# A routed layer on one Trainium2 core: the table of tokens and weights moves into four extra columns of each routed row

## Chip, cores and metric

The kernel runs on one core of one Trainium2 chip. The metric is the device time of one execution in microseconds (us), lower is better.

## What is computed

The reference is a transformer layer on 8192 tokens (16 sequences of 512) of width 256, all in float32:

```python
x = L0_attn_inputs_q
xn = _layernorm(x, axis=-1)
x = x + attn(xn) + ffn(xn)
```

`attn` is linear attention with 16 heads. `ffn` is a shared SwiGLU block plus a routed part: each token picks one of two groups of four experts, then the best two experts in it, with a weight for each.

```python
h = _swiglu(flat @ w1.T)
for e in range(NUM_EXPERTS):
    routed = routed + h * w_se[:, e:e + 1] @ w2[e].T
```

So every token has one hidden row `h` of 512 numbers, two experts and two weights.

## The kernel before

**Matmuls.** Each float32 operand is split into a high part and a low part, and each product is made of three matmuls (`mm3`, lines 341 to 343). TensorE (PE) does little else.

**First phase, 16 batches of 512 tokens** (`batch` on each engine, unrolled for the first and the last, a loop between). In one batch PE computes keys, values, queries, the shared hidden layer and the routed hidden layer, and closes with the output products `y` (lines 599 to 615). VectorE (DVE) makes `kb`, the routing (`probabilities`, `best_two`, `ranks_in`, `table_rows`) and all gates. The two experts of a token form one of 12 classes. `ranks_in` gives each token its place in the list of its class, so `pos_i` is its row in a DRAM table with room for `CAP` = 8320 rows in each class. Two DRAM tensors are filled at that row by GpSimd (POOL), with indirect transfers of 128 rows each:

- `tab_d` takes 16 bytes per token: token number, two weights, a zero (tile `rows`);
- `h_d` takes the hidden row, 2048 bytes (buffers `hs[t]`, which lie over `phik` and `expt`).

POOL's order in a batch is written by hand. In the first batch it is: `low(0)`, `low(1)`, the split of `w_out`, four table scatters (line 1222), `reciprocal_root(1)`, `biased()` (adds the bias to the residual, line 1200), four row scatters (line 1228), `low(2)`, `low(3)`. The functions `low` make `h_lo` (line 1176), which PE needs for `y`. In the later batches `reciprocal_root` and `biased` stand at the start of the batch.

The next batch's normalised input `xn` goes to DRAM and back in another layout on the SP queue (lines 394 and 397), and DVE transposes it into `xT` (`x_transposed`, line 840), which lies over `phik`; so `x_transposed` waits for two things: the loads of line 397 (`xn_ld`) and the landing of the four row scatters (`hs_st`). After `xT` SP loads the input of the batch after (line 377), DVE takes its statistics (`norm`, line 809) and only then does `base` and `k_in` (line 940).

**Unused rows.** The second phase works on tiles of 128 rows, and the last tile of a class is only partly filled. So `tab_d` is filled at the start, 13 transfers of a constant (token 8192, which is out of bounds and is skipped), lines 366 to 368, on the SP queue behind the weights; and `h_d` gets 13 transfers of zeros behind the end of each class, in the last batch (line 412).

**Second phase, 75 tiles of 128 rows.** Each tile has one pair of experts. SP (first half) and ScalarE (ACT, second half) load a tile of `h_d` in four pieces of 128 x 512 bytes (`pieces`, line 348), DVE transposes it (line 1096), ACT makes the high part, DVE the low part (line 1102), PE multiplies with both experts, DVE scales with the weights (`add`, lines 1128 and 1130), POOL adds the rows to `out` with an indirect transfer (line 1274). The weights and tokens of a tile come with a load of 128 x 16 bytes from `tab_d` (line 432). SP works in groups of four tiles, and a group begins with a wait for the table loads of the groups before:

```python
def tiles_in(q):
    wait_apart(sp, tab_ld, 16 * TB * q)
```

Of the kernel before, what the change touches and what calls it, by code (L numbers as in the profile page):

```python
# [6 lines left out]
def layer_program(nc, x, w_k, w_v, w_q, w_o, w_in, w_out, w_exp, w_rt, b_q, b_kl, b_o,  # L7
# [7 lines left out]
    P = 128  # L15
# [19 lines left out]
    ROWS = SENT + P  # L35
    H1 = 512
    W1 = 2 * 1024
    UNIT = E * HC * D // B
# [4 lines left out]

    h_d = nc.dram_tensor("h_d", (ROWS, H1), f32, kind="Internal").ap()
    tab_d = nc.dram_tensor("tab_d", (ROWS, 4), i32, kind="Internal").ap()
    xn_d = nc.dram_tensor("xn_d", (S, D), f32, kind="Internal").ap()

    ctx = ExitStack()
    with ctx:
# [6 lines left out]
        def pair(name, shape):  # L56
# [16 lines left out]
        kb = sb("kb", [P, TB, D], f32)  # L73
        expt = sb("expt", [P, 2, 512], f32)
        relut = sb("relut", [P, 2, 512], f32)
        phik = sb("phik", [P, TB, D], f32)
        v = sb("v", [P, TB, DC, QG, HP + 1], f32)
# [59 lines left out]
        tok = sb("tok", [P, TB], f32)  # L137
        rows = sb("rows", [P, TB, 4], i32)

        fill = wexp_hi[:, W1 + B * UNIT - 4 * CAP // P:].bitcast(i32).rearrange("p (n w) -> p n w", w=4)  # L140
        cnt_i = sb("cnt_i", [P, NSLOT], i32)
# [6 lines left out]
        ends = wstage[0:1, 4 * NT:4 * NT + NSLOT].bitcast(i32)  # L148
        zeros = wstage[:, 512:1024]
        tab = wstage[:, 0:4 * NT].bitcast(i32).rearrange("p (n w) -> p n w", w=4)  # L150
        cur = sb("cur", [P, 2, TB, 4], i32)
        idx_cur = sb("idx_cur", [P, 2, TB], i32)

        hs = [phik[:, 0:2, :].rearrange("p t d -> p (t d)"), phik[:, 2:4, :].rearrange("p t d -> p (t d)"),
              expt[:, 0, :], expt[:, 1, :]]

        xn_blocks = xt[:, :, :].rearrange("p t d -> p (t d)").rearrange("p (b c k) -> p b c k", c=DC, k=32)
        xT = phik[:, :, :].rearrange("p t d -> p (t d)").rearrange("p (c s) -> p c s", c=DC)

# [33 lines left out]
        w_ld = sem("w_ld")  # L193
        fill_st = sem("fill_st")

# [3 lines left out]
        w1_split = sem("w1_split")  # L199
        fill_set = sem("fill_set")  # L200
        const_set = sem("const_set")
# [64 lines left out]
        hlo_rdy = sem("hlo_rdy")  # L266
        row_st = sem("row_st")
        hs_st = sem("hs_st")
# [83 lines left out]
        def _(sp):  # L352
# [11 lines left out]

            sp.wait_ge(fill_set, 2)
            for c in range(NCLS):
                sp.dma_start(tab_d[c * CAP:(c + 1) * CAP, :].rearrange("(p n) w -> p n w", p=P), fill[:, :, :]).then_inc(fill_st, 16)
            sp.dma_start(tab_d[SENT:ROWS, :], fill[:, 0, :]).then_inc(fill_st, 16)

            def load(b, last):  # L370
# [30 lines left out]

            sp.wait_ge(zero_set, 1)
            sp.wait_ge(ends_rdy, 1)
            for n in range(NCLS + 1):
                if n < NCLS:
                    g, k = divmod(n, NCLS // 2)
                    j, i = PAIRS[k]
                    end = sp.value_load(ends[0:1, 16 * g + 4 * j + i:16 * g + 4 * j + i + 1], min_val=0, max_val=SENT)
                    tail = bass.ds(end, P)
                else:  # L410
                    tail = slice(SENT, ROWS)
                sp.dma_start(h_d[tail, :], zeros).then_inc(zero_st, 16)

            sp.wait_ge(wexp_split, B)
            sp.wait_ge(infoi_rdy, 1)
            sp.wait_ge(zero_st, 16 * (NCLS + 1))
            sp.wait_ge(fill_st, 16 * (NCLS + 1))
            sp.wait_ge(row_st, 16 * TB * B)
            sp.wait_ge(hs_st, 16 * TB * B)
            sp.wait_ge(xT_rdy, 2 * (B - 1))  # L420

            def tiles_in(q):

                wait_apart(sp, tab_ld, 16 * TB * q)
                rows_at = rows_of(mybir.EngineType.SP, q * TB, TB)
                for t in range(TB):
                    at = rows_at[t]
                    if first_row(q) and t == 2:
                        sp.wait_ge(qlo_rdy, DC * B)
                    wait_apart(sp, tr_done, TB * q + t - 3)  # L430
                    pieces(sp, at, t, 0)
                    sp.dma_start(tab[:, bass.ds(q * TB + t, 1), :].rearrange("p t w -> p (t w)"),
                                 tab_d[bass.ds(at, P), :]).then_inc(tab_ld, 16)

# [7 lines left out]
        def _(pe):  # L442
            def first_transposes():

                pe.wait_ge(stay_ld, 16)
                for t in range(TB):
                    pe.wait_ge(xn_rdy, t + 1)
                    for c in range(DC):
                        mm = pe.transpose(bank[2 + 2 * c][:, t * P:(t + 1) * P], phik[:, t, c * P:(c + 1) * P], ident)
                        if t == TB - 1:  # L450
                            mm.then_inc(t_done, 1)
# [27 lines left out]
            def batch(b, last):  # L479
# [37 lines left out]
                for c in range(DC):  # L517
                    for t in range(TB):
                        for n in range(QG):
                            at = c * P + n * HP  # L520
                            mm = pe.matmul(bank[2][n * HP:(n + 1) * HP, c * (HP + 1):(c + 1) * (HP + 1)], phik[:, t, at:at + HP],
                                           v[:, t, c, n, :], start=(c == 0 and t == 0), stop=(t == TB - 1), skip_group_check=True)
# [264 lines left out]
        def _(dve):  # L787
# [30 lines left out]
            def first_normalise():  # L818
                dve.wait_ge(rstd_rdy, 1)
                for t in range(TB):  # L820
                    dve.tensor_scalar(phik[:, t, :].rearrange("p (c i k) -> p c i k", c=DC, k=32),
                                      xt[:, t, :].rearrange("p (i c k) -> p c i k", c=DC, k=32),
# [85 lines left out]
            def table_rows(b):  # L908

                wait(dve, row_st, 16 * TB * b)  # L910
                wait(dve, hs_st, 16 * TB * b)
# [23 lines left out]
            def batch(b, last):  # L935
# [7 lines left out]
                def phi_k(i):  # L943
                    dve.wait_ge(ek_rdy, 2 * b + i + 1)
                    wait(dve, acc_done, b)
                    wait(dve, hs_st, 16 * TB * b)
                    dve.scalar_tensor_tensor(phik[:, 2 * i:2 * i + 2, :].rearrange("p t n -> p (t n)"),
                                             kb[:, 2 * i:2 * i + 2, :].rearrange("p t n -> p (t n)"), 0.0,
# [212 lines left out]
        def _(pool):  # L1161
            pool.memset(fill[:, :, 1:4], 0).then_inc(fill_set, 1)
            pool.memset(fill[:, :, 0:1], N).then_inc(fill_set, 1)
            pool.memset(mhalf[:, :], -0.5).then_inc(pool_set, 1)
# [27 lines left out]
            def batch(b, last):  # L1192
# [15 lines left out]
                if last:  # L1208
                    pool.wait_ge(wexp_split, B)
                    pool.memset(zeros, 0.0).then_inc(zero_set, 1)  # L1210
                low(0, HC * b, hhi_rdy, hlo_rdy)
                low(1, HC * b + 1, hhi_rdy, hlo_rdy)

                if first_row(b):
# [3 lines left out]
                    low_part(wstage[:, :], wout_hi_, wout_lo_, ffn_split)  # L1218
                    pool.wait_ge(fill_st, 16 * (NCLS + 1))
                wait_apart(pool, row_rdy, b + 1)  # L1220
                for t in range(TB):
                    scatter(tab_d, rows[:, t, :], t, row_st)
                if first_row(b):
                    reciprocal_root(1)
                    biased()
                for t in range(TB):
                    wait_apart(pool, rg_rdy, TB * b + t + 1)
                    scatter(h_d, hs[t], t, hs_st)
                low(2, HC * b + 2, hhi_rdy, hlo_rdy)
# [132 lines left out]
```

## Time and profile before

| | us |
|---|---|
| median of 3 runs | 936.19 |
| lowest, highest | 934.6, 937.14 |
| the profiled execution, its own time | 936.16 |
| its span, first to last instruction | 934.3 |

The mean granted TensorE clock over the span is 0.989 of full speed. The profile is one execution; the span leaves out 1.9 us that lie around it. Times in its rows count from the start of the span.

### The profile page before, as it was taken

What the parts mean: (1) busy time and instruction counts of PE and PEld (TensorE: products, weight loads), DVE (VectorE), ACT (ScalarE), POOL (GpSimd) and SP (SyncE); (2) the same over time, 40 slices, a digit from 0 to 9 for tenths busy, and PEclk for the clock granted to TensorE, in tenths of its full rate; (3) what the DMA queues carried; (4) which work ended last, traced back from release to release, by engine and by line L of the source; (5) the groups of instructions that cost most, each with busy time, mean ns of one, the idle gap of its engine ahead of it and who ended that gap; (6) DMA issues with size and microseconds to landing.
All of it is one profiled execution on the core that took longest, in us unless ns stands there. A gap on an engine that the chain in (4) does not pass through costs nothing. (4 is left out here: it accounts for less than half of the span.)

```text
span 934.3 us, 22822 instructions
## 1 busy us (share of the span) xinstructions
PE 907.5 (97%) x6974; PEld 818.6 (88%) x6975; DVE 697.6 (75%) x1819; ACT 363.4 (39%) x596; POOL 464.9 (50%) x554
## 2 busy tenths in 40 slices
PE   7879999999999999999999999999989999999995
PEld 7678989898898989898888989898969999999995
DVE  5958687877878686877778786877675877777773
ACT  4425445344535345454435354453431222222220
POOL 4754364535354453635253543645352556655564
PEclk8999999999999999999999999999999999999998
DMA  9133324241313224241313223241155777787760
GB/s 277 59 113 103 123 61 138 61 123 68 101 68 101 93 76 146 57 134 48 120 68 101 90 79 131 60 134 55 60 192 132 144 136 142 144 151 137 136 125 1
DMA packets 145912, 100.21 MB, mean 107 GB/s; under 512 B 55520, under 2 KB 136928, under 8 KB 145888
## 3 DMA queue, kind: packets, MB, share of 16 engines
q1 hardware_dynamic: 105600, 64.08, 24.0%
q0 software_dynamic: 17968, 25.32, 12.6%
q10 hardware_dynamic: 22320, 10.51, 4.1%
q8 instruction: 13, 0.21, 0.1%
q14 instruction: 11, 0.09, 0.0%
HBM read 53.29 MB, written 48.00 MB: 108 GB/s over the span
## 5 line engine op out<-in xcount | busy, mean ns | idle before, releaser
L341 PE MATMUL bank<-wexp_hi,xnT_hi 128*128 (+1 forms) x560 | 191.1, 341 | 2.3 <-DVE phik L933 1.6
L343 PE MATMUL bank<-wexp_hi,xnT_lo 128*128 (+1 forms) x560 | 186.1, 332 | 0.0
L342 PE MATMUL bank<-wexp_lo,xnT_hi 128*128 (+1 forms) x560 | 185.8, 332 | 0.0
L1176 POOL TENSOR_TENSOR h_lo<-gated,h_hi 128x256 fp32r<-128x256 f32 x128 | 97.1, 779 | 104.0 <-ACT h_hi L683 103.6
L341 PEld LDWEIGHTS bank<-wexp_hi,xnT_hi 128*128 128x128 f32 x560 | 106.3, 190 | 15.7 <-issue 4.2
L343 PEld LDWEIGHTS bank<-wexp_hi,xnT_lo 128*128 128x128 f32 x560 | 106.3, 190 | 10.7
L342 PEld LDWEIGHTS bank<-wexp_lo,xnT_hi 128*128 128x128 f32 x560 | 106.4, 190 | 9.6
L341 PE MATMUL bank<-xnT_hi,win_hi 128*128 128x512 f32 x256 | 102.4, 400 | 3.1 <-DVE expt L933 3.1
L1200 POOL TENSOR_TENSOR res<-res,bo_t 128x256 f32<-128x256 f32 x64 | 47.2, 766 | 113.5 <-DMA res<-x 113.5
L343 PE MATMUL bank<-xnT_hi,win_lo 128*128 128x512 f32 x256 | 100.4, 392 | 0.0
L342 PE MATMUL bank<-xnT_lo,win_hi 128*128 128x512 f32 x256 | 100.3, 392 | 0.0
L341 PE MATMUL bank<-wexp_hi,h_hi 128*128 x296 | 83.4, 282 | 0.1
L343 PE MATMUL bank<-wexp_hi,h_lo 128*128 x296 | 83.3, 281 | 0.0
L342 PE MATMUL bank<-wexp_lo,h_hi 128*128 x296 | 83.2, 281 | 0.0
L1274 POOL DMA_INDIRECT out<-res,idx_cur x39 | 61.4, 1574 | 42.2 <-DVE res L1130 31.4
L1195 POOL DMA_INDIRECT tab_d<-rows,pos_i x64 | 63.2, 987 | 37.9 <-DVE tok L925 21.2
L683 ACT CAST h_hi<-gated 128x512 fp32r<-128x512 f32 x64 | 39.7, 620 | 108.0 <-DVE gated L929 108.0
L341 PE MATMUL bank<-wout_hi,h_hi 128*128 128x256 f32 x256 | 72.9, 285 | 3.7 <-POOL h_lo L1176 3.7
L929 DVE TENSOR_TENSOR gated<-gated,bank 128x512 f32<-128x512 f32 x64 | 43.9, 685 | 43.7 <-ACT gated L679 43.7
L341 PE MATMUL bank<-wkv_hi,xnT_hi 128*128 128x266 f32 (+1 forms) x256 | 73.9, 289 | 2.5 <-DVE xnT_lo L834 1.3
L342 PE MATMUL bank<-wkv_lo,xnT_hi 128*128 128x266 f32 (+1 forms) x256 | 73.4, 287 | 0.0
L343 PE MATMUL bank<-wkv_hi,xnT_lo 128*128 128x266 f32 (+1 forms) x256 | 73.3, 286 | 0.0
(191 smaller groups left out, 2417.2 us busy)
## 6 DMA issues: line engine op xcount, KB each, us to landing
res<-x SPq DMA_DIRECT2D x16, 512.0 KB, 3.6
out<-res SPq DMA_DIRECT2D x16, 512.0 KB, 3.0
xt<-x SPq DMA_DIRECT2D x15, 512.0 KB, 3.5
xn_d<-xt SPq DMA_DIRECT2D x15, 512.0 KB, 4.7
xt<-xn_d SPq DMA_DIRECT2D x60, 128.0 KB, 3.2
xt<-h_d SPq DMA_DIRECT2D x76, 64.0 KB
xt<-h_d ACTq DMA_DIRECT2D x76, 64.0 KB
kb<-h_d SPq DMA_DIRECT2D x76, 64.0 KB
```

The lines of the kernel that those rows point to most:

```text
L341: e.matmul(to, w_hi, m_hi_, start=first_, stop=False, skip_group_check=free)
L342: e.matmul(to, w_hi, m_lo_, start=False, stop=False, skip_group_check=free)
L343: return e.matmul(to, w_lo, m_hi_, start=False, stop=last_, skip_group_check=free)
L683: act.copy(h_hi[:, j, :], gated[:, j % 2, :]).then_inc(hhi_rdy, 1)
L929: dve.tensor_tensor(gated[:, j % 2, :], gated[:, j % 2, :], bank[up_bank][:, :], ALU.mult).then_inc(gate_rdy, 1)
L1176: ins = pool.tensor_tensor(h_lo[:, j, cols], gated[:, j % 2, cols], h_hi[:, j, cols].bitcast(f32), ALU.subtract)
L1195: pool.indirect_dma_start(d, bass.IndirectOffsetOnAxis(ap=pos_i[:, t:t + 1], axis=0), src, None).then_inc(done, 16)
L1200: ins = pool.tensor_tensor(res[:, t, :], res[:, t, :], bo, ALU.add)
L1274: pool.indirect_dma_start(out, bass.IndirectOffsetOnAxis(ap=idx_cur[:, t // TB, t % TB:t % TB + 1], axis=0), ring[t], None, bounds_check=N ...
```

## The change

The row of `h_d` grows from 512 to 516 numbers. Columns 512 to 515 hold what `tab_d` held. In SBUF one tile `hrow` of 4 x 516 numbers per partition takes the place of `phik`, `expt` and `rows`. One indirect transfer writes hidden row, token and weights. `tab_d`, its fill and the four table scatters of each batch are gone. The transfers behind the ends of the classes write rows of 516 numbers, whose token is 8192 and whose other numbers are zero. The second phase reads the pieces and the table entries from the wider rows. The diff, cut to its core (names of `phik[:, t, ...]` that become `phik(t)[:, ...]` are left out):

```diff
+    HR = H1 + 4
...
-    h_d = nc.dram_tensor("h_d", (ROWS, H1), f32, kind="Internal").ap()
-    tab_d = nc.dram_tensor("tab_d", (ROWS, 4), i32, kind="Internal").ap()
+    h_d = nc.dram_tensor("h_d", (ROWS, HR), f32, kind="Internal").ap()
...
-        expt = sb("expt", [P, 2, 512], f32)
+        hrow = sb("hrow", [P, TB, HR], f32)
+        expt = hrow[:, 2:4, 0:H1]
...
-        rows = sb("rows", [P, TB, 4], i32)
+        rows = hrow[:, :, H1:HR].bitcast(i32)
...
-        zeros = wstage[:, 512:1024]
+        tails = wstage[:, 1024 - HR:1024]
...
+        hs = [hrow[:, t, 0:H1] for t in range(TB)]
+        def phik(t):
+            return hrow[:, t // 2, (t % 2) * D:(t % 2 + 1) * D]
...
-        xT = phik[:, :, :].rearrange("p t d -> p (t d)").rearrange("p (c s) -> p c s", c=DC)
+        xT = hrow[:, 0:DC, 0:S]
...
-            sp.wait_ge(fill_set, 2)
-            for c in range(NCLS):
-                sp.dma_start(tab_d[c * CAP:(c + 1) * CAP, :].rearrange("(p n) w -> p n w", p=P), fill[:, :, :]).then_inc(fill_st, 16)
-            sp.dma_start(tab_d[SENT:ROWS, :], fill[:, 0, :]).then_inc(fill_st, 16)
...
-                sp.dma_start(h_d[tail, :], zeros).then_inc(zero_st, 16)
+                sp.dma_start(h_d[tail, :], tails).then_inc(zero_st, 16)
...
                     sp.dma_start(tab[:, bass.ds(q * TB + t, 1), :].rearrange("p t w -> p (t w)"),
-                                 tab_d[bass.ds(at, P), :]).then_inc(tab_ld, 16)
+                                 h_d[bass.ds(at, P), H1:HR].bitcast(i32)).then_inc(tab_ld, 16)
...
-            pool.memset(fill[:, :, 1:4], 0).then_inc(fill_set, 1)
-            pool.memset(fill[:, :, 0:1], N).then_inc(fill_set, 1)
...
-                    pool.memset(zeros, 0.0).then_inc(zero_set, 1)
+                    pool.memset(tails[:, 0:H1], 0.0).then_inc(zero_set, 1)
+                    pool.memset(tails[:, H1:H1 + 1].bitcast(i32), N).then_inc(zero_set, 1)
+                    pool.memset(tails[:, H1 + 1:HR], 0.0).then_inc(zero_set, 1)
...
-                    pool.wait_ge(fill_st, 16 * (NCLS + 1))
                 wait_apart(pool, row_rdy, b + 1)
-                for t in range(TB):
-                    scatter(tab_d, rows[:, t, :], t, row_st)
...
-                    scatter(h_d, hs[t], t, hs_st)
+                    scatter(h_d, hrow[:, t, :], t, hs_st)
```

## Rows read from the trace of the kernel before

**Rows 1.** Page, busy time of TensorE.

```profile
PE 907.5 (97%) x6974; PEld 818.6 (88%) x6975; DVE 697.6 (75%) x1819; ACT 363.4 (39%) x596; POOL 464.9 (50%) x554
```

**Rows 2.** Waits of PE: in total, times, longest.

```profile
PE bank L341 <- POOL h_lo L1176: 3.7, 1, 3.7
...
PE bank L341 <- DVE lg L941: 1.2, 1, 1.2
...
PE bank L341 <- DVE xnT_lo L1102: 0.7, 1, 0.7
```

**Rows 3.** Page, costliest groups: the table scatters.

```profile
L1195 POOL DMA_INDIRECT tab_d<-rows,pos_i x64 | 63.2, 987 | 37.9 <-DVE tok L925 21.2
```

**Rows 4.** Timeline of POOL, first batch: start, duration, what, idle before.

```profile
41.22 1.21 POOL L1195 DMA_INDIRECT tab_d<-rows,pos_i  x1 [0.18 <-issue]
...
47.37 3.02 POOL L1200 TENSOR_TENSOR res<-res,bo_t 128x256 f32<-128x256 f32 x4
...
54.75 0.96 POOL L1195 DMA_INDIRECT h_d<-expt,pos_i  x1 [0.30 <-issue]
```

**Rows 5.** Timeline of DVE, first batch and start of the second.

```profile
43.52 0.69 DVE L1015 TENSOR_TENSOR qn_hi<-relut,stay 128x512 fp32r<-128x512 f32 x1
...
47.42 3.12 DVE L828 TENSOR_SCALAR xt<-xt,mv,rstd 128x256 f32<-128x256 f32 x4
...
60.47 1.30 DVE L840 STREAM_TRANSPOSE phik<-xt 128x512 f32<-128x512 f32 x2 [7.45 <-DMA h_d<-expt,pos_i]
...
68.80 0.42 DVE L940 TENSOR_TENSOR kb<-bank,bkl 128x256 f32<-128x256 f32 x1
```

**Rows 6.** Line 828 in all batches: min/median/max ns.

```profile
L828 DVE TENSOR_SCALAR xt<-xt,mv,rstd x60: 402/405/880, 47.4 to 621.4; 128x256 f32<-128x256 f32 x60
```

**Rows 7.** Timeline of the SP queue, first batch.

```profile
50.57 0.38 SPq L394 DMA_DIRECT2D xn_d<-xt  x1
53.53 2.09 SPq L397 DMA_DIRECT2D xt<-xn_d  x4
62.03 0.41 SPq L377 DMA_DIRECT2D xt<-x  x1
```

**Rows 8.** DMA issues, 53.5 to 61 us: count, KB, median us to landing.

```profile
xt<-xn_d SPq DMA_DIRECT2D x4, 128.0 KB, 4.3
```

**Rows 9.** The same, 161 to 167 us, a middle batch.

```profile
xt<-xn_d SPq DMA_DIRECT2D x4, 128.0 KB, 3.1
```

**Rows 10.** Windows: busy us (instructions) by engine, PEclk, DMA share, GB/s.

```profile
57.20:59.90 2.70, 2.70 (x12) 2.70 (x13) 0.00 (x0) 0.00 (x0) 2.62 (x5) 0.50 0.82 188
```

**Rows 11.** The same for 40 us of the second phase.

```profile
760.00:800.00 40.00, 40.00 (x338) 40.00 (x337) 30.10 (x57) 8.69 (x14) 26.85 (x22) 1.00 0.76 140
```

**Rows 12.** Timeline of the SP queue, second phase.

```profile
723.96 0.88 SPq L348 DMA_DIRECT2D xt<-h_d  x2
...
780.66 0.86 SPq L348 DMA_DIRECT2D xt<-h_d  x2
...
787.01 0.37 SPq L432 DMA_DIRECT2D wstage<-tab_d  x1
...
791.58 0.86 SPq L348 DMA_DIRECT2D xt<-h_d  x2
...
823.28 0.86 SPq L348 DMA_DIRECT2D xt<-h_d  x2
```

**Rows 13.** Timeline of DVE, second phase, two tiles eight apart.

```profile
781.43 0.49 DVE L1128 TENSOR_SCALAR res<-bank,cur 128x256 f32<-128x256 f32 x1 [0.68 <-PE bank L343]
...
804.32 0.48 DVE L1128 TENSOR_SCALAR res<-bank,cur 128x256 f32<-128x256 f32 x1 [0.68 <-issue]
```

**Rows 14.** Waits of the SP queue from 716 to 925 us.

```profile
SPq L293 <- DMA wstage<-tab_d: 35.1, 15, 3.1
```

**Rows 15.** DMA issues, 2 to 8.3 us, two loads at the start.

```profile
expt<-w_q SPq DMA_DIRECT2D x1, 256.0 KB, 4.2
...
bkl<-b_kl SPq DMA_DIRECT2D x1, 133.0 KB, 4.0
```

More of the change, by code:

```diff
@@ L73, in layer_program @@
         kb = sb("kb", [P, TB, D], f32)
-        expt = sb("expt", [P, 2, 512], f32)
+        hrow = sb("hrow", [P, TB, HR], f32)
+        expt = hrow[:, 2:4, 0:H1]
         relut = sb("relut", [P, 2, 512], f32)
-        phik = sb("phik", [P, TB, D], f32)
         v = sb("v", [P, TB, DC, QG, HP + 1], f32)
@@ L137, in layer_program @@
         tok = sb("tok", [P, TB], f32)
-        rows = sb("rows", [P, TB, 4], i32)
-        fill = wexp_hi[:, W1 + B * UNIT - 4 * CAP // P:].bitcast(i32).rearrange("p (n w) -> p n w", w=4)
+        rows = hrow[:, :, H1:HR].bitcast(i32)
         cnt_i = sb("cnt_i", [P, NSLOT], i32)
@@ L152, in layer_program @@
         idx_cur = sb("idx_cur", [P, 2, TB], i32)
-        hs = [phik[:, 0:2, :].rearrange("p t d -> p (t d)"), phik[:, 2:4, :].rearrange("p t d -> p (t d)"),
-              expt[:, 0, :], expt[:, 1, :]]
+        hs = [hrow[:, t, 0:H1] for t in range(TB)]
+        def phik(t):
+            return hrow[:, t // 2, (t % 2) * D:(t % 2 + 1) * D]
         xn_blocks = xt[:, :, :].rearrange("p t d -> p (t d)").rearrange("p (b c k) -> p b c k", c=DC, k=32)
-        xT = phik[:, :, :].rearrange("p t d -> p (t d)").rearrange("p (c s) -> p c s", c=DC)
+        xT = hrow[:, 0:DC, 0:S]
         hb = [xt[:, 0:2, :].rearrange("p t d -> p (t d)"), xt[:, 2:4, :].rearrange("p t d -> p (t d)"),
@@ L193, in layer_program @@
         w_ld = sem("w_ld")
-        fill_st = sem("fill_st")
         w_round = sem("w_round")
@@ L199, in layer_program @@
         w1_split = sem("w1_split")
-        fill_set = sem("fill_set")
         const_set = sem("const_set")
@@ L266, in layer_program @@
         hlo_rdy = sem("hlo_rdy")
-        row_st = sem("row_st")
         hs_st = sem("hs_st")
@@ L400, in _ @@
             rounds(sp, load, B)
-            sp.wait_ge(zero_set, 1)
+            sp.wait_ge(zero_set, 3)
             sp.wait_ge(ends_rdy, 1)
@@ L416, in _ @@
             sp.wait_ge(zero_st, 16 * (NCLS + 1))
-            sp.wait_ge(fill_st, 16 * (NCLS + 1))
-            sp.wait_ge(row_st, 16 * TB * B)
             sp.wait_ge(hs_st, 16 * TB * B)
@@ L448, in first_transposes @@
                     for c in range(DC):
-                        mm = pe.transpose(bank[2 + 2 * c][:, t * P:(t + 1) * P], phik[:, t, c * P:(c + 1) * P], ident)
+                        mm = pe.transpose(bank[2 + 2 * c][:, t * P:(t + 1) * P], phik(t)[:, c * P:(c + 1) * P], ident)
                         if t == TB - 1:
@@ L520, in batch @@
                             at = c * P + n * HP
-                            mm = pe.matmul(bank[2][n * HP:(n + 1) * HP, c * (HP + 1):(c + 1) * (HP + 1)], phik[:, t, at:at + HP],
+                            mm = pe.matmul(bank[2][n * HP:(n + 1) * HP, c * (HP + 1):(c + 1) * (HP + 1)], phik(t)[:, at:at + HP],
                                            v[:, t, c, n, :], start=(c == 0 and t == 0), stop=(t == TB - 1), skip_group_check=True)
@@ L820, in first_normalise @@
                 for t in range(TB):
-                    dve.tensor_scalar(phik[:, t, :].rearrange("p (c i k) -> p c i k", c=DC, k=32),
+                    dve.tensor_scalar(phik(t).rearrange("p (c i k) -> p c i k", c=DC, k=32),
                                       xt[:, t, :].rearrange("p (i c k) -> p c i k", c=DC, k=32),
@@ L908, in table_rows @@
             def table_rows(b):
-                wait(dve, row_st, 16 * TB * b)
                 wait(dve, hs_st, 16 * TB * b)
@@ L946, in phi_k @@
                     wait(dve, hs_st, 16 * TB * b)
-                    dve.scalar_tensor_tensor(phik[:, 2 * i:2 * i + 2, :].rearrange("p t n -> p (t n)"),
+                    dve.scalar_tensor_tensor(hrow[:, i, 0:H1],
                                              kb[:, 2 * i:2 * i + 2, :].rearrange("p t n -> p (t n)"), 0.0,
```

## Prediction

> **What bounds the kernel.** I read the busy shares first: TensorE (PE) is busy 907.5 us of 934.3 [rows 1]. So a change elsewhere can win only where PE stands still, about 27 us in all, or lose by making it stand still. The waits of PE say who holds it. One wait belongs to work that this change shortens: 3.7 us for `h_lo` from POOL [rows 2]. The others come from DVE; 1.2 us for `lg` of line 941 stands soon after, and 0.7 us for `xnT_lo` of line 1102 at the start of the second phase [rows 2]. In the middle batches PE has no wait that is listed. So the 64 table scatters, 63.2 us of POOL [rows 3], are covered by PE in 15 of 16 batches, and the question is the first batch and the second phase.
>
> **The first batch, what is removed.** Before, POOL starts the table scatters at 41.22 and ends the last row scatter at 55.7 [rows 4]; only then can `low(2)` run, and PE waits for it. The four scatters go, at 0.99 each with 0.3 between, about 5.1 us. POOL's later work moves up by that: `biased()` from 47.37 to about 42.2, the last row scatter ends at about 50.6, and its data lands near 53. `low(2)` then waits for the gates of DVE and not for POOL, and PE's 3.7 us wait goes. The twelve matmuls behind it ran at a granted clock of 0.50, the lower level of 1.2 GHz, in 2.70 us [rows 10], where 2.4 GHz needs half of that; that loss of 1.3 us goes too. If nothing else were in the way, PE would reach the second batch 5 us earlier.
>
> **What is late next.** PE can't begin the second batch without `xT`, and `k_in` of that batch stands behind a chain that begins with it: transpose at 60.47 [rows 5], load of the next input issued at 62.03 [rows 7], statistics, `base`, `k_in` at 68.80 [rows 5], and PE's 1.2 us wait ends there. So the gain is what the transpose gains. It waited for the row scatters until 60.47, which move up to 53. But it also waits for the four loads of line 397: issued from 53.53 for 2.09 us [rows 7], with 4.3 us to landing beside the row scatters [rows 8], so the last lands at about 59.5. Without the scatters beside them they need 3.1 [rows 9], which takes 1.2 us off.
>
> The loads begin when `normalise` (line 828) has ended and the store has landed. Before, `normalise` ran beside `biased()`: four instructions took 3.12 us [rows 5], where the median of one is 0.405 [rows 6], so about 1.5 us of it was waiting for POOL. Now `biased()` lies at 42.2 to 45.2, beside other DVE work. If that work took no harm, `normalise` would end 1.5 us earlier. But lines 1011, 1013 and 1015 stand there, the last at 43.52 [rows 5], and if each is held by a POOL instruction as line 828 was, by about 0.37 us, DVE loses 1.1 of the 1.5 again. I take 0.4 net. The Trainium skill ("SBUF — State Buffer", on the shared port pair) says that a DVE instruction with two SBUF inputs or in a two-port mode and a POOL instruction exclude each other for a whole instruction. By that rule all three of the lines collide, which is the 0.4; without it the gain would be 1.5.
>
> So the loads start 0.4 earlier and land 1.2 faster. The last lands at about 57.9 and the transpose starts at about 58.0 instead of 60.47: 2.45 us. PE is ready for the second batch at about 60.2, gets its input at 60.7, runs to 64.4 and then waits for `k_in` until 66.9, a wait of 2.5 us in place of 1.2. A wait of 3.7 was followed by half clock that cost 1.3 [rows 2, 10], one of 1.2 by no such stretch; for 2.5 I put 0.6, bounds 0 and 1.3. Net gain of the first batch: 2.45 - 0.6 = 1.85 us. Bounds: 0.9 - 1.3 = -0.4 (the loads still land at 59.5, and the clock is lost), and 3.6 (all of the 1.5, no clock lost).
>
> **Edits that I cost at nothing.** The fill transfers stand on SP's queue behind all the weights, and no wait of PE ends on a DMA; the two memsets and POOL's wait for the fill lie where POOL waits for others. The freed POOL time of the middle batches (5.1 us each) is covered by PE; if PE's cover were gone it would be worth as much each. The tails' rows of 2064 bytes add 0.8% of bytes and two small memsets, about five us before POOL's next work. `hrow` changes addresses, not shapes, of DVE and ACT operands. The row scatter of 2064 bytes is one instruction as before; POOL took the same time for 16 and for 2048 bytes per row (0.99 and 0.96) [rows 3, 4], so 16 more cost it nothing.
>
> **The second phase, what is moved.** This is where it can lose. Every tile is read in pieces of 512 bytes whose rows now lie 2064 apart and start at odd multiples of 16 bytes, and 128 entries of 16 bytes are read from 128 rows instead of one block of 2 KB. The DMA engines are at 0.76 there [rows 11]. Who waits for them? SP. A group of four tiles is issued from 780.66 to 787.4, and the next starts at 791.58 [rows 12]: 4.2 us for the table load to land, and this is SP's main wait, 35.1 us in 15 times [rows 14]. Nine groups from 723.96 to 823.28 [rows 12] took 11.04 each. PE needs 22.89 us for eight tiles [rows 13], 11.45 for four. So SP's loop is faster than PE by only 0.4 us a group. If a table load lands up to 0.4 later, PE notices nothing; each us beyond that costs 17 us over the 17 groups left, less a lead of about 2 us. At the start of this phase there is no lead: PE waits 0.7 there for the first tile of the second group [rows 2].
>
> Bounds for the added landing. Below: nothing; the load of `b_kl`, whose rows lie 1064 bytes apart, landed in 4.0 us beside 4.2 for an aligned load of twice the size [rows 15], so no harm shows. A gain is not excluded, but PE would not see it. Above: the DMA share can only grow to 1.0, a factor 1.32, which makes 4.2 into 5.5, plus 1.3. I take plus 0.3, nearer to the lower row: it stays below 0.4, and costs about 0.3 once, at the start. The sum: 936.16 - 1.85 + 0.3 = 934.6, against the profiled execution's own time, which equals the median of the runs within 0.1.
>
> **Rivals.** (1) Slower: table loads and pieces land later by more than 0.4 us, and SP's loop paces PE. With 1.0 us more a group takes 12.04, 0.6 over PE: 17 x 0.6 = 10, less 2 of lead, so plus 8, and the time is 942.6; at the upper bound 1.3 it is 948. For it: the thin 0.4, and that landing is the wait. Against: the `b_kl` row. The Trainium skill ("DMA: Bandwidth & Descriptors", How a descriptor splits into AXI transactions) says that a read which doesn't start on 256 bytes fetches from the boundary below, which speaks against this change; by its beats of 32 bytes a piece would cost about 28% more on average, an estimate. No row here shows it. (2) Faster: the collision of `biased()` is not repeated and the clock holds, or PE's 3.7 us are won in full: 3.6 to 5 us less, 931.9. For it: the row of line 1015 lies only at the edge of the new place. Against: line 828. (3) The freed POOL time is hidden altogether, because the loads of line 397 land no earlier: 936.2.
>
> **How the numbers follow.** My case (932.8 to 936.5) has 0.42, rival 3 0.09, rival 2 0.23, rival 1 0.26. 0.3% is 2.8 us, about what a measurement can tell here: faster means below 933.4, slower above 939.0. My case gives faster in one of ten, rival 2 nearly always (0.04 + 0.21 = 0.25); rival 1 stays within 0.3% in a quarter of its cases (slower 0.20); the rest, 0.55, is no change. The range runs from 931.5 to 943.5.
>
> **What would show it.** Right: no PE wait for `h_lo` in the first batch; the transpose at about 58, released by the loads of `xn_d` and not by the scatters; a PE wait of 2 to 3 us for `lg`; lines 1011 to 1015 at 43 to 45 us longer than their 0.69 and less; groups of SP 11.0 to 11.4 apart. Wrong: groups more than 11.5 apart with waits of PE for line 1102 (rival 1), or a transpose before 57.3 (rival 2).

## The result and the profile after

The changed kernel takes 928.34 us (median of 6 runs, 925.83 to 931.09) against 936.38 for the kernel before on the same chip (6 runs, 934.6 to 937.55). The ratio is 0.9913, 95% interval 0.9893 to 0.9933: 8.1 us less, where 1.6 us less was predicted, and outside the range. In the profiled executions the span fell from 934.3 to 926.2.

The page's busy times of the kernel after, to be read beside [rows 1]:

```profile
PE 899.9 (97%) x6974; PEld 810.6 (88%) x6975; DVE 694.2 (75%) x1819; ACT 363.6 (39%) x596; POOL 401.8 (43%) x490
```

This line holds the surprise. TensorE (PE) executes the same 6974 matmuls, and is busy 7.6 us less. Idle time is span less busy time: 26.8 us before, 26.3 after. So nearly all of the gain lies where the prediction had nothing, in the duration of matmuls that the diff does not touch. Groups of PE by tile and form, 725 to 900 us (second phase), of the kernel before; the columns are busy time, mean ns of one, and idle time before:

```profile
L341 PE MATMUL bank<-wexp_hi,xnT_hi 128*128 x245 | 69.3, 283 | 0.0
L341 PE MATMUL bank<-wexp_hi,h_hi 128*128 x245 | 68.9, 281 | 0.0
L343 PE MATMUL bank<-wexp_hi,h_lo 128*128 x244 | 68.7, 282 | 0.0
```

The same of the kernel after:

```profile
L339 PE MATMUL bank<-wexp_hi,xnT_hi 128*128 x248 | 70.2, 283 | 0.0
L341 PE MATMUL bank<-wexp_hi,h_lo 128*128 x253 | 69.9, 276 | 0.0
L339 PE MATMUL bank<-wexp_hi,h_hi 128*128 x252 | 69.6, 276 | 0.0
```

In this phase the tiles of routed rows rest in `xnT` and `h` by turns, and meet the expert weights in `wexp`. Only the matmuls on `h` got faster. Their recorded time overlaps with the next one, so what counts is the distance from start to start: 118.5 ns became 113, and a tile of 24 matmuls 2.72 us instead of 2.84, while tiles on `xnT` stay at 2.88. Line 1118 of DVE, which starts when a tile is done, shows the pattern 2.72, 2.88, 2.88, 2.72:

```profile
782.73 0.48 DVE L1118 TENSOR_SCALAR res<-bank,cur 128x256 f32<-128x256 f32 x1 [0.70 <-PE bank L341]
785.45 0.48 DVE L1118 TENSOR_SCALAR res<-bank,cur 128x256 f32<-128x256 f32 x1 [0.62 <-PE bank L341]
788.33 0.48 DVE L1118 TENSOR_SCALAR relut<-bank,cur 128x256 f32<-128x256 f32 x1 [0.78 <-PE bank L341]
791.21 0.48 DVE L1118 TENSOR_SCALAR relut<-bank,cur 128x256 f32<-128x256 f32 x1 [0.77 <-issue]
793.93 0.48 DVE L1118 TENSOR_SCALAR relut<-bank,cur 128x256 f32<-128x256 f32 x1 [0.63 <-PE bank L341]
```

PE's stretch from the first to the last matmul of the second phase is 210.3 us instead of 216.0 (5.7 less). From the start of the third batch to the start of the last it is 550.5 instead of 551.8 (1.3 less; the matmuls of `wout` on `h` went from 284 to 280 ns). What is left of the 8.1 us is 0.4 in the first two batches, 0.1 in the last and 0.65 behind the last matmul. Not all of the 5.7 is the pace of tiles: 37 tiles on `h` at 0.12 us each are 4.4, and a second profile of the same kernel (e12, below) has 211.8 us in this stretch.

What moved `h`? `rows` lay behind `h_hi` and `h_lo` in SBUF, 64 bytes per partition. Now these 64 bytes are part of `hrow`, which lies ahead of them. So every tile behind `hrow` starts 64 bytes further on, and those ahead stay. Modulo 256 bytes, by the program's allocation, `wexp` and `xnT` start at 64 before and after, `h_hi` and `h_lo` at 192 before and at 0 after.

**The first batch** of the kernel after. Waits of PE from 40 to 112 us:

```profile
PE bank L339 <- DVE xnT_lo L837: 2.0, 1, 2.0
PE bank L339 <- DVE lg L931: 1.9, 1, 1.9
PE bank L339 <- DVE hrow L923: 1.7, 1, 1.7
```

The wait for `h_lo` of [rows 2] is gone; in its place stand 2.0 us for the transposed input of the second batch, and more for `lg`. POOL's timeline (start, duration), beside [rows 4]:

```profile
42.56 2.87 POOL L1188 TENSOR_TENSOR res<-res,bo_t 128x256 f32<-128x256 f32 x4
...
49.92 0.96 POOL L1183 DMA_INDIRECT h_d<-hrow,pos_i  x1 [0.30 <-issue]
```

DVE's, beside [rows 5]:

```profile
43.25 0.84 DVE L1001 CAST relut<-relut 128x128 fp32r<-128x128 f32 x1
44.12 0.72 DVE L1003 SCALAR_TENSOR_TENSOR relut<-relut,stay 128x128 f32<-128x128 f32 x1
44.88 1.10 DVE L1005 TENSOR_TENSOR qn_hi<-relut,stay 128x512 fp32r<-128x512 f32 x1
...
48.89 1.46 DVE L819 TENSOR_SCALAR xt<-xt,mv,rstd 128x256 f32<-128x256 f32 x4
...
60.11 1.30 DVE L831 STREAM_TRANSPOSE hrow<-xt 128x512 f32<-128x512 f32 x2 [6.41 <-DMA xt<-xn_d]
```

And that of the SP queue, beside [rows 7]:

```profile
50.38 0.39 SPq L387 DMA_DIRECT2D xn_d<-xt  x1
54.32 1.92 SPq L390 DMA_DIRECT2D xt<-xn_d  x4
```

POOL's work moved up as predicted (the last row scatter ends at 50.9, 50.6 predicted), `normalise` lost its collision (1.46 us for the four, not 3.12), lines 1001, 1003 and 1005 gained one each (0.84, 0.72 and 1.10 us; before, as lines 1011, 1013 and 1015, 0.23, 0.35 and 0.69), and the transpose is now released by the loads of `xn_d`. But it starts at 60.11 and not at 58.0.

**The second phase.** The SP queue, beside [rows 12], and its wait, beside [rows 14]:

```profile
786.72 0.82 SPq L346 DMA_DIRECT2D xt<-h_d  x2
...
793.10 0.37 SPq L423 DMA_DIRECT2D wstage<-h_d  x1
797.18 0.82 SPq L346 DMA_DIRECT2D xt<-h_d  x2
```

```profile
SPq L291 <- DMA wstage<-h_d: 37.3, 17, 2.7
```

The last table load of a group lands 3.7 us after its issue is done, not 4.2 as in [rows 12]. Over ten groups from 722 us on, the median is 3.6 us, 4.0 before and 3.8 in e12, so reading the 128 rows cost nothing; a gain is not shown. There was also less to lose than predicted: in both traces a table load goes as 128 packets of 16 bytes (7936 of them before and 8217 after on SP's queue from 730 to 900 us), so the 2 KB that lay in one block were not read as one. Ten groups from 722.60 to 827.87 took 10.5 us each (11.0 in e12), against PE's 11.2 for four tiles. So rival 1, SP as the bound, is out, though in e12 by little. The DMA engines do pay. Windows of 40 us (columns as in [rows 10]), beside [rows 11], where the share was 0.76:

```profile
760.00:800.00 40.00, 40.00 (x345) 40.00 (x344) 31.23 (x60) 9.31 (x15) 25.34 (x23) 1.00 0.84 146
```

### The profile page after: what moved, and what is told of

Read it like the earlier page. It is cut to its first block and busy times, and to the rows that moved or that the text cites. A ratio compares the mean times of both kernels' runs of the same rounds, so it can differ in the third digit from the quotient of the medians.

```text
span 926.2 us, 22745 instructions
## 1 busy us (share of the span) xinstructions
PE 899.9 (97%) x6974; PEld 810.6 (88%) x6975; DVE 694.2 (75%) x1819; ACT 363.6 (39%) x596; POOL 401.8 (43%) x490
## 5 line engine op out<-in xcount | busy, mean ns | idle before, releaser
L341 PEld LDWEIGHTS bank<-wexp_hi,xnT_lo 128*128 128x128 f32 x560 | 106.4, 190 | 10.5
L1183 POOL DMA_INDIRECT h_d<-hrow,pos_i x64 | 63.3, 989 | 82.7 <-DVE hrow L923 52.5
L341 PE MATMUL bank<-wout_hi,h_lo 128*128 128x256 f32 x256 | 71.6, 280 | 0.0
```

Of the source, the lines that this page charges most:

```text
L341: return e.matmul(to, w_lo, m_hi_, start=False, stop=last_, skip_group_check=free)
L1183: pool.indirect_dma_start(d, bass.IndirectOffsetOnAxis(ap=pos_i[:, t:t + 1], axis=0), src, None).then_inc(done, 16)
```

## The experiments

Each was timed against the kernel before on the same chip. "Starts at 64" and the like always means the byte address of a tile within a partition, modulo 256.

### Is it the address of h?

Two kernels exchange the position of `h`, and with it that of all tiles from `relut` on, by unused bytes alone: 192 ahead of `relut` bring `h` back to 192 in the kernel after (e1), 64 bring it to 0 in the kernel before (e2).

```diff
+        sb("pad0", [P, 48], f32)      # e1, kernel after
...
+        sb("pad0", [P, 16], f32)      # e2, kernel before
         relut = sb("relut", [P, 2, 512], f32)
```

Expected of e1:

> The changed kernel with 192 unused bytes put behind hrow, so that h_hi, h_lo, qn, gated and all that follows start again at 192 modulo 256 bytes in each partition, as in the kernel before; nothing else differs. Address theory: the six us that the second phase gained belong to the start of h_hi and h_lo in SBUF, so tiles 2 and 3 of four go back from 2.72 to 2.85 us each, and the time rises by 7 us to about 935.5. Rival (less traffic of POOL and DMA makes the second phase faster): the time stays at 928.

Expected of e2:

> The kernel before, with its table, fill and table scatters, and 64 unused bytes put ahead of relut, so that h_hi, h_lo and all that follows start at 0 modulo 256 bytes as in the changed kernel. Address theory: the time falls by about 7 us to 929 to 930 without any of the change. Rival: it stays at 936.

e1 took 932.35 us against 936.75, ratio 0.9958 (0.9945 to 0.9972); e2 took 929.81, ratio 0.9923 (0.9910 to 0.9936). Busy times and two groups (725 to 900 us) of e1:

```profile
PE 907.4 (98%) x6974; PEld 817.9 (88%) x6975; DVE 695.3 (75%) x1819; ACT 363.7 (39%) x596; POOL 403.2 (43%) x490
...
L340 PE MATMUL bank<-wexp_hi,h_hi 128*128 x247 | 69.5, 282 | 0.0
...
L340 PE MATMUL bank<-wexp_hi,xnT_hi 128*128 x240 | 68.2, 284 | 0.7 <-DVE xnT_lo L1093 0.6
```

Groups of e2:

```profile
L342 PE MATMUL bank<-wexp_hi,h_hi 128*128 x256 | 70.7, 276 | 0.0
...
L342 PE MATMUL bank<-wexp_hi,xnT_hi 128*128 x245 | 69.4, 283 | 0.0
```

The kernel before, with 64 unused bytes and not a line of the change, has the fast matmuls and 7.2 us of gain; the kernel after with `h` put back has PE's old busy time (907.4). That settles where the miss came from. The change without its addresses is worth 0.0042, 3.9 us (935.5 was expected of e1, not 932.35), and this too is more than the 1.6 predicted. Whether the two add is not settled: 0.9958 times 0.9923 is 0.9881, and the kernel after has 0.9913 (0.9893 to 0.9933), or 0.9892 (0.9872 to 0.9912) on another chip (below).

### Which address rule?

In the next two every tile of 512 bytes or more starts at 0 modulo 128 (e3; all the operands of this phase at 128), or `xnT` alone moves, to 128 (e4).

```diff
...
+            pad = -at[0] % 128 if big else 0      # e3, in sb()
+            if pad:
+                ctx.enter_context(nc.sbuf_tensor("pad_" + name, [P, pad // 4], f32))
...
+        sb("pad0", [P, 16], f32)                  # e4
         xnT_hi, xnT_lo = pair("xnT", [P, DC, S])
+        sb("pad1", [P, 48], f32)
```

Expected of e3:

> The changed kernel with unused bytes ahead of every tile of 512 bytes or more, so that each starts on a multiple of 128 bytes; most, h_hi, xnT_hi and wexp_hi too, lie at 128 modulo 256. If 128 is the step that matters, the h tiles stay at 2.72 us and the xnT tiles fall from 2.88 to 2.72, and the first phase gains as well: 928 less 5 to 10, about 921. If 256 is the step, h loses its place and nothing is won: about 935. Traffic rival: 928.

Expected of e4:

> The changed kernel with xnT_hi and xnT_lo alone moved by 64 bytes, to 128 modulo 256; h stays at 0 and the expert weights, the moving side in the second phase, stay at 64. If the start of the loaded weights (the stationary side) counts in steps of 128, the xnT tiles of the second phase fall from 2.88 to 2.72 us, 37 x 0.15 = 5.6 us less, about 922. If the moving side counts, or the step is 256: 928.

e3 took 933.73 us, ratio 0.9968 (0.9957 to 0.9980); e4 927.09, 0.9885 (0.9870 to 0.9899). A group of e3 (725 to 900 us), then two of e4, and one of e4's first phase (80 to 680 us):

```profile
L350 PE MATMUL bank<-wexp_hi,h_hi 128*128 x247 | 69.9, 283 | 0.0
```

```profile
L341 PE MATMUL bank<-wexp_hi,xnT_hi 128*128 x259 | 71.5, 276 | 0.0
...
L341 PE MATMUL bank<-wexp_hi,h_hi 128*128 x256 | 70.7, 276 | 0.0
```

```profile
L341 PE MATMUL bank<-wexp_hi,xnT_hi 128*128 128x512 f32 x228 | 94.3, 414 | 0.0
```

Being well aligned is no help: with all operands at the same phase every tile takes 2.88 us. With `xnT` at 128 and `h` at 0, both 64 away from `wexp`, every tile takes 2.72. What counts is the distance between the stationary and the moving operand. The price is in the first phase: its matmuls of 512 columns on the same two tiles took 414 and 395 ns instead of 409 and 390, and a batch 42.6 us instead of 42.35, so e4 gains little in sum (922 was expected).

e5 moves `wexp` instead, to 128, so that the distances change places: `h` at 0 is now 128 away, `xnT` at 64 is 64 away.

```diff
+        sb("pad0", [P, 16], f32)
         wexp_hi, wexp_lo = pair("wexp", [P, W1 + B * UNIT])
+        sb("pad1", [P, 48], f32)
```

> The kernel after, with the two expert weight tiles 64 bytes further on in each partition (128 modulo 256, the other tiles as they were: xnT 64, h 0). Theory (what counts is the distance modulo 128 bytes between the stationary and the moving operand of a 256-column matmul, 0 is slow and 64 fast): the matmuls of the second phase on h now lie at distance 0 and go from 276 back to about 282 ns, those on xnT at distance 64 fall from 283 to about 276, so the tiles of the second phase trade places (about 2.85 us for those now at 2.72, and the reverse), and the total is about 928, up to 931 if the 512-column matmuls of the first phase pay for the distance of 64 as they did when xnT was moved. Rival (the address of the moving or the stationary tile alone counts, not the distance): the h matmuls keep 276 ns and the xnT ones 283, no tile changes its pace, about 928.

It took 930.74 us, ratio 0.9942 (0.9924 to 0.9961). Groups, 725 to 900 us:

```profile
L341 PE MATMUL bank<-wexp_hi,h_hi 128*128 x253 | 71.2, 282 | 0.0
...
L341 PE MATMUL bank<-wexp_hi,xnT_hi 128*128 x240 | 67.2, 280 | 0.1
```

Half a success. The `h` matmuls went back to 282 without having been moved, so it isn't the absolute address that counts. But those on `xnT` fell to 280 only, tiles of 2.82 us, where the rule said 276 and 2.72. e9 and e10 ask why. e9 moves `h` (and what lies behind `relut`) to 192 as well; e10 shifts the hi weights against the lo ones by 256 bytes, and nothing modulo 256.

```diff
+        sb("pad2", [P, 48], f32)      # e9, on top of e5
         relut = sb("relut", [P, 2, 512], f32)
...
+        sb("pad2", [P, 64], f32)      # e10, on top of e5
+        wexp_hi = sb("wexp_hi", [P, W1 + B * UNIT], f32r)
+        sb("pad3", [P, 64], f32)
+        wexp_lo = sb("wexp_lo", [P, W1 + B * UNIT], f32r)
```

Expected of e9:

> The kernel with the expert weights at 128 (where the tiles on xnT took 2.83 us instead of the 2.72 of the rule), and h_hi, h_lo and what lies behind them moved to 192 modulo 256. Rule of the distance modulo 128: the h tiles (distance 64) go to 2.72 us. What is open is the xnT tiles, whose own distance does not change. If they fall to 2.72 too, where h lies matters for matmuls that do not read it, and the kernel comes to about 924 to 926; if they stay at 2.83, it is where the hi and lo weights lie to each other, and the kernel comes to about 926 to 928.

Expected of e10:

> The kernel with the expert weights at 128, with wexp_hi another 256 bytes on, so that the hi and lo weights lie 256 apart modulo 512 (as in the kernel with all pairs at distance 64, which had every tile at 2.72); modulo 256 nothing moves. If the phase modulo 512 of hi against lo matters, the xnT tiles fall from 2.83 to 2.72 us while the h tiles stay at 2.85 (distance 0 modulo 128), about 928.5. If only phases modulo 256 matter, both keep 2.83 and 2.85, about 930.7.

e9 took 925.73 us, ratio 0.9869 (0.9845 to 0.9893), e10 930.48, 0.9915 (0.9894 to 0.9936). A group of e9, then one of e10, 725 to 900 us:

```profile
L342 PE MATMUL bank<-wexp_hi,xnT_hi 128*128 x257 | 71.1, 277 | 0.1
```

```profile
L344 PE MATMUL bank<-wexp_hi,xnT_hi 128*128 x240 | 67.3, 280 | 1.1 <-DVE xnT_lo L1097 1.0
```

The offset of hi to lo does nothing. Moving `h` makes the matmuls on `xnT` fast, though they don't read `h`. All kernels together (start modulo 256; time of one tile, us):

| kernel | wexp | xnT | h | tile on xnT | tile on h |
|---|---|---|---|---|---|
| before, e1, e6 | 64 | 64 | 192 | 2.88 | 2.84 |
| after, e2, e7, e11, e12 | 64 | 64 | 0 | 2.88 | 2.72 |
| e3 | 128 | 128 | 128 | 2.88 | 2.88 |
| e4 | 64 | 128 | 0 | 2.72 | 2.72 |
| e5, e10 | 128 | 64 | 0 | 2.82 | 2.85 |
| e9, e8 (below) | 128 | 64 | 192 | 2.72 | 2.72 |

Every fast tile has its two operands 64 apart modulo 128; equal or 128 apart was slow each time. Row e5 is the one exception in the other direction: 64 apart is needed, but was not enough while `h` lay 128 from `wexp`. Why is not shown. That it is `h` itself, and not one of the tiles that move with it in e9, is narrowed down by the next kernel.

### The rule put to use

e8 is the kernel after with padding alone, so that the pairs of the matmuls of 256 columns on `h`, on the routed rows in `xnT` and on `qn` (with `m`) lie 64 apart modulo 128, and `wexp` and `xnT` in the 512-column ones at distance 0. For that the expert weights need another phase than the first layer's weights in the same tile: 16 unused columns between them.

```diff
+    W1S = W1 + 16
...
-                            off = at[n] + (W1 + j * D)
+                            off = at[n] + (W1S + j * D)
...
+        sb("pad0", [P, 16], f32)      # ahead of wout: 128
+        sb("pad1", [P, 48], f32)      # ahead of wexp: 64, its experts 128
+        wexp_hi = sb("wexp_hi", [P, W1S + B * UNIT], f32r)
+        sb("pad2", [P, 48], f32)
+        wexp_lo = sb("wexp_lo", [P, W1S + B * UNIT], f32r)
+        sb("pad3", [P, 48], f32)      # xnT stays at 64
...
+        sb("pad4", [P, 48], f32)      # ahead of h: 192
+        sb("pad5", [P, 32], f32)      # ahead of m: 64
```

> The kernel after, with padding alone: each pair of stationary and moving tiles that meet in 256-column matmuls (second phase wexp with xnT and with h, and the output's wout with h) at a distance of 64 modulo 128 bytes, the pairs of the 512-column matmuls at a distance of 0. Theory of the distance: all tiles of the second phase at 2.72 us instead of the mix of 2.72 and 2.88 (another 3.6 us, as the kernel with xnT moved showed) and no loss of 3 us in the first phase, about 921 to 924. Rival (absolute addresses or bank conflicts of another sort): 927 or more, with tiles at 2.83 to 2.88 left in the second phase.

It took 922.63 us against 936.13, ratio 0.9857 (0.9842 to 0.9872). Its busy times and a group (725 to 900 us), and one of 80 to 680 us:

```profile
PE 895.7 (97%) x6974; PEld 806.1 (88%) x6975; DVE 696.4 (76%) x1819; ACT 363.7 (40%) x596; POOL 408.4 (44%) x490
...
L347 PE MATMUL bank<-wexp_hi,xnT_hi 128*128 x256 | 71.1, 278 | 0.6 <-DVE xnT_lo L1100 0.5
```

```profile
L347 PE MATMUL bank<-wexp_hi,xnT_hi 128*128 128x512 f32 x235 | 95.9, 408 | 0.0
```

This beats both kernels, by addresses alone: about 5 us under the kernel after (0.9857 against 0.9909 for e7, which takes as long as the kernel after and ran on the same chip; 5.7 by the medians). The 512-column matmuls kept their 408, where e4 had 414. Two more things stand in this trace. The matmuls of `m` on `qn`, 64 apart here, took 279 ns, and 281 to 284 in before, after, e3 and e5, where they lie at distance 0: a third pair that follows the rule. And in the second phase e8 has the positions of e9, with `relut`, `qn` and `gated` where e5 has them. If the other paddings of e8 don't matter, that leaves, of the tiles that e9 moved, `h` and what lies behind it (`m` and on) for the exception of e5.

### What is the order of the scatters worth?

e6 is the kernel before in which only the first batch's four table scatters move behind `low(3)`, so that they no longer stand ahead of the row scatters and of `h_lo`. e11 is the same with `h` at 0.

```diff
-                for t in range(TB):
-                    scatter(tab_d, rows[:, t, :], t, row_st)
+                if not first_row(b):
+                    for t in range(TB):
+                        scatter(tab_d, rows[:, t, :], t, row_st)
...
+                    for t in range(TB):
+                        scatter(tab_d, rows[:, t, :], t, row_st)
```

Expected of e6:

> The kernel before, where the table's four scatters of the first batch alone are issued behind the first layer's last expert step instead of ahead of the routed rows' use; no tile moves. Theory (the first batch's part of the change is worth a little): TensorE's wait for h_lo in the first batch is gone and the batch ends 0.4 to 1.5 us earlier, 935 to 936 against 936.4. Rival (what is left of the gain beside the addresses sits in the queue of POOL): about 932, as the kernel after with h moved back gives 932.35.

Expected of e11:

> The kernel before with both of what is held to make the result: h_hi and h_lo 64 bytes on (alone 929.81, 0.9923) and the first batch's table scatters behind the last expert step of the first layer (alone 934.38, 0.9977). The table, its fill and the scatters of the other batches stay. If the two effects add, 936.4 * 0.9923 * 0.9977, about 927 to 928.3, as the kernel after: what else the change removes would then be worth nothing. Rival: the gone table and its fill give something of their own, and this one stays at 929 or more.

e6 took 934.38 us, ratio 0.9977 (0.9966 to 0.9989): about 2.2 us, by the median 1.75, a little above the 0.4 to 1.5 that were expected, and about half of e1's gain. The waits of PE from 60 to 76 us show the predicted exchange, 2.5 us for `lg` and none for `h_lo`:

```profile
PE bank L341 <- DVE lg L941: 2.5, 1, 2.5
PE bank L341 <- DVE xnT_lo L846: 0.7, 2, 0.5
```

But the profile does not place the gain there. Up to the start of the third batch e6 is 0.7 us behind the kernel before (1.5 behind already at line 1011, which the edit does not reach, and 0.9 won after it). Its 2.1 us of shorter span come from the last batch (1.4, where the clock held, see below) and the second phase (1.2). So the exchange of waits is shown; what it is worth is shown less well.

e11 was a miss: 931.91 us against 938.42 on that chip, ratio 0.9934 (0.9915 to 0.9953), where 0.990 was expected. Waits of PE from 112 to 660 us, a stretch in which neither the kernel before nor e2 nor e6 has any:

```profile
PE bank L342 <- POOL h_lo L1177: 1.5, 5, 0.3
```

In e11 POOL holds PE up in the middle batches: table scatters, row scatters and then `h_lo` stand in its queue. The batches took 42.25 to 42.86 us, 553.6 for thirteen against 550.5 in e2, which is about what is missing; 1.5 of these 3 us are the listed wait, and the rest I can't place. e2 has the same queue in these batches and no such wait, so POOL seems to sit at the edge there; what tipped it over in e11 is not shown. The 5.1 us of POOL that the change removes from each middle batch were costed at nothing because PE covered them; by this one profile that cover is thin.

### Do the unaligned rows cost?

In e7 a routed row has 576 numbers in DRAM, 2304 bytes, so that each starts on a multiple of 256 bytes; the tiles in SBUF keep their phase.

```diff
-    HR = H1 + 4
+    HR = H1 + 64
...
-                                 h_d[bass.ds(at, P), H1:HR].bitcast(i32)).then_inc(tab_ld, 16)
+                                 h_d[bass.ds(at, P), H1:H1 + 4].bitcast(i32)).then_inc(tab_ld, 16)
```

> The kernel after, where each routed row in DRAM is 576 numbers long instead of 516 with its four extra columns (2304 bytes, so that every row begins at a multiple of 256 bytes), tiles in SBUF kept at the same phase. Theory (rows that begin off the line make the reads of the second phase cost 17% more of the DMA engines, hidden behind TensorE): the queue q10 falls from 4.8% of the span back to about 4.1%, the time stays at 928. Rival (the longer DMA time of unaligned rows is on the path, in the landing of the groups of four tiles): the time falls by 1 us or more.

It took 928.08 us, ratio 0.9909 (0.9894 to 0.9923), as the kernel after. The page's row of ACT's queue, which reads half of the pieces (packets, MB, share of 16 engines), of before, after and e7:

```profile
q10 hardware_dynamic: 22320, 10.51, 4.1%
```

```profile
q10 hardware_dynamic: 22320, 10.51, 4.8%
```

```profile
q10 hardware_dynamic: 22320, 10.51, 4.4%
```

Per packet (share times 16 times span over packets) that is 27.5, 31.9 and 29.2 ns: rows off the 256-byte line cost 16% more DMA time than before, aligned but further apart 6%. The second is near the noise: counted packet by packet the kernel before has 27.2, and e2, which reads the same rows, 28.2. Packets of 512 bytes alone, from 730 to 900 us on this queue, took 28.9, 34.5 and 30.8 ns in the mean, and 27 in the median each time: the cost falls on some packets, not on all. All of it is hidden behind PE.

### A second profile of the kernel after

> The kernel after, unchanged, for a second profile: if the landing of the last loads for the transpose at 60.11 us was one late packet, they land at about 58 this time and the wait on xnT_lo (2.0 us) falls to about 0.4; if it belongs to the kernel it stays. The same for the granted clock behind the idle stretch of the last batch (0.61 in 691:694, where two other kernels kept 1.00). The time stays at 928.3.

It took 928.25 us, ratio 0.9892 (0.9872 to 0.9912). The transpose of the first batch:

```profile
59.89 1.30 DVE L831 STREAM_TRANSPOSE hrow<-xt 128x512 f32<-128x512 f32 x2 [6.21 <-DMA xt<-xn_d]
```

So the late landing came twice in this kernel. It does not belong to the change, though: in e1, e4 and e9, which differ from the kernel after by padding alone, the transpose starts at 57.90, 58.20 and 58.22. Windows of e1, after and e12 (granted clock is the number behind POOL's), in the last batch, right behind a wait of 2.9, 3.0 and 2.9 us for line 923 (924 in e1) that all of them have:

```profile
691.00:694.00 3.00, 3.00 (x18) 2.16 (x17) 1.61 (x4) 1.81 (x3) 1.26 (x2) 1.00 0.83 315
```

```profile
691.00:694.00 3.00, 3.00 (x10) 2.32 (x9) 1.38 (x3) 1.22 (x2) 1.19 (x2) 0.61 0.88 329
```

```profile
691.00:694.00 3.00, 3.00 (x7) 2.35 (x8) 2.21 (x4) 1.22 (x2) 1.92 (x2) 0.50 0.73 279
```

After the same idle stretch the clock fell to its lower level of 1.2 GHz for some 3 us in ten of the fourteen profiles, and stayed at 2.4 GHz in e1, e3, e6 and e11. From the start of the last batch to the second phase e1 took 46.25 us and the kernel after 47.8. These 1.5 us explain why single profiles don't add up to better than that, and a part of e1's 3.9. The clock held in two of the four profiles with the table's scatters and in two of the ten without them, which is no sign that the change helps it.

## Why the prediction was wrong, step by step

**The step that failed** is the sentence "`hrow` changes addresses, not shapes, of DVE and ACT operands", costed at nothing. It asked which engines read the new tile, and forgot the tiles behind it. The allocation moved 64 bytes from behind `h` to ahead of it, and `h` is an operand of PE, which is 97% busy. e2 measures this term alone at 7.2 us (0.9923), against a whole result of 8.1. No row in the profile of before said so, yet two hinted at it: matmuls of one shape on `xnT` and on `h` had means of 283 and 281 to 282 ns.

**What bounds the kernel** was read rightly, and the conclusion from it was too narrow. A change elsewhere can win only PE's idle 27 us as long as PE's work is the same; here its duration changed.

**The first batch**: predicted 1.85 us. The mechanism was right: the wait for `h_lo` went, the loads of `xn_d` became the release, and `lg` was next. The sizes were off. The transpose started at 60.11 (59.89 in e12), not 58.0: the store landed 3.9 us after its issue and not 3.0 as before, and the last of the four loads landed 3.9 us after the issue, though their median was the predicted 3.1. `normalise` ended 0.2 earlier, for which I took 0.4, and all three lines collided with `biased()` as argued, for 1.4 us in sum where I took 1.1. The loss of clock behind the `lg` wait, 0.6 predicted, didn't occur in the kernel after, and did in e12, the same kernel (0.50 from 69 to 72 us), as in e1 and e6.

The profiles differ by up to 1.8 us before the change can act, so the first batches are better counted from line 1011 (1001 in the kernel after). The stretches of the span, in us; a batch starts with PE's first matmul on `wkv`:

| stretch | before | after | e12 | e1 | e2 | e6 |
|---|---|---|---|---|---|---|
| up to line 1011 | 42.9 | 43.2 | 43.8 | 43.1 | 43.3 | 44.4 |
| to the third batch | 65.6 | 64.8 | 65.2 | 63.8 | 65.4 | 64.7 |
| to the last batch | 551.8 | 550.5 | 550.6 | 551.8 | 550.5 | 551.7 |
| last batch | 47.9 | 47.8 | 48.8 | 46.3 | 47.9 | 46.5 |
| second phase, to the last matmul | 216.0 | 210.3 | 211.8 | 215.9 | 211.9 | 214.9 |
| behind it | 10.1 | 9.5 | 9.5 | 9.5 | 10.1 | 10.1 |

So the term of 1.85 measured 0.8 in the kernel after and 0.4 in e12, 1.8 in e1, and between 0.4 and 2.3 in all ten profiles with the change: the forecast lies inside, above most of them. By time, e6 gives 1.75 to 2.2 us for the reordering alone, with the table kept. This holds the 1.85, but only 0.9 of it stands in these rows of e6's profile, so the agreement may be luck.

**The middle batches**: "covered by PE" holds in the kernel before and in e2, with no wait in these batches. e11 suggests that the cover is thin: five waits of 0.3 us.

**The second phase**: the predicted added landing of 0.3 us did not come; by the medians it was 0.4 shorter in the kernel after and 0.1 in e12. SP's loop stayed ahead of PE. The estimate from the Trainium skill ("DMA: Bandwidth & Descriptors", How a descriptor splits into AXI transactions), about 28% more for a piece, pointed the right way: the trace has 16%, in DMA time that nobody waits for. The 28% counted rows at odd multiples of 16 bytes alone. Rows 2064 bytes apart start at every multiple of 16 modulo 256, and the same count of beats then gives 25%, still an estimate.

**Outside the terms**: behind the last matmul the kernel after needs 0.65 us less. All of it is the `DRAIN` with which POOL ends the program. Before, then after (min/median/max ns, start):

```profile
L49 POOLq DRAIN  x1: 4682/4682/4682, 929.4 to 929.4; - x1
```

```profile
L49 POOLq DRAIN  x1: 4029/4029/4029, 921.9 to 921.9; - x1
```

It took 4682 ns in all four profiles with the table and 4029 in all ten with the change. The change removes 64 of POOL's transfers and three semaphores; which of them shortens the drain, if either does, no run shows.

**What stays open**: how much of the 3.9 us of the change at unmoved `h` (e1) would come back in other executions. In e1's profile they are 1.5 up to the third batch, 1.6 in the last batch, where the clock held, 0.65 in the drain and 0.1 in the second phase; the first varies between profiles by more than 1 us, the second is luck of the clock, and only the drain is the same each time. And why an `h` that is not read slows the matmuls on `xnT` in e5.

## What to carry to other kernels

Where one engine is 97% busy, compare its operands' addresses first: any edit that adds, drops or resizes an SBUF tile moves all tiles behind it, and here 64 unused bytes were worth more than the edit itself. To time an edit fairly, hold the addresses of the busiest engine's operands with padding, and try the phases on purpose once (e8 won about 5 us more). And a queue whose work is called covered should be given with its margin: POOL's had none to spare in e11, where waits appeared that e2 with the same queue doesn't have.

## What the hardware showed that I had not expected

In these kernels a matmul's pace depends on how its two operands lie to each other in SBUF. Matmuls of 256 columns started 113 ns apart where stationary and moving operand were 64 bytes apart modulo 128, and 118 to 120 ns where they were equal or 128 apart. One case breaks this: in e5 and e10 a pair at 64 took 118. Only distances in steps of 64 were tried; `wkv`, whose rows of 2088 bytes give others, is not sorted by this. Matmuls of 512 columns went the other way, by some 5 ns in e4 (409 and 414 for the first of three) and by 1 to 3 ns in e5, e9 and e10, at the same distance. 113 against 120 is 6%, on an engine that is 97% busy. I have no mechanism for it that a run has shown.
